# Transposing the normalised activations by DMA instead of by TensorE, in the QKV stage of an attention and mixture-of-experts layer

## What is computed

```
h = layernorm(x)
q, k, v = split(h @ w_qkv + b_qkv)            # 16 heads of 64
q = elu(q) + 1 ;  k = elu(k) + 1
kv  = sum over tokens of k^T v                # per head, 64 x 64
z   = 1 / (q . sum over tokens of k)
x = x + ((q @ kv) * z) @ w_proj + b_proj
h = layernorm(x)
gates = sinkhorn((h @ router_w^T + router_b) / temperature), 3 iterations, top 2 of 8
x = x + sum over experts of gate * (relu(h @ wg) * (h @ wp)) @ wo
```

## Time and profile before

| | |
|---|---|
| time, median of 2 runs | 7586.61 us (7111.52 and 8061.7) |
| the profiled execution | 7111.29 us |
| its span, first to last instruction, slowest core | 7109.5 us |
| the other cores' spans | 7101.5 to 7107.5 us |
| TensorE busy | 6254.6 us (88%) |
| VectorE busy | 2794.3 us (39%) |
| ScalarE busy | 839.1 us (12%) |

### The profile page before, as it was taken

How to read it: one execution, slowest core, us unless ns; L and a number is a source line. 1 busy time by engine, 2 the same in 40 slices (tenths; PEclk the granted TensorE clock), 3 DMA queues, 4 the chain that set the end, 5 groups by cost and what they waited for, 6 DMA issues and landing times.

```text
span 7109.5 us, 77888 instructions; the slowest of 8 cores (7101.5 to 7109.5 us)
## 1 busy us (share of the span) xinstructions
PE 6254.6 (88%) x29238; PEld 2744.0 (39%) x29238; DVE 2794.3 (39%) x5085; ACT 839.1 (12%) x1390; POOL 165.5 (2%) x202
## 2 busy tenths in 40 slices
PE   4777655589999999999999998999999999999999
PEld 1222222234444444444444443444444444444444
DVE  3444444433333333333333333333333333333334
ACT  1111111111111111111111110111111111111110
POOL 0000000000000000000000000000000000000000
PEclk9888766689999999999999999999999999999999
DMA  4000111142222222222222244222222222222222
GB/s 80 24 21 24 36 54 54 54 89 36 36 36 36 36 36 36 36 36 36 36 36 36 36 81 85 36 36 36 36 36 36 36 36 36 36 36 36 36 36 66
DMA packets 192672, 298.65 MB, mean 42 GB/s; under 512 B 5930, under 2 KB 137002, under 8 KB 192306
## 3 DMA queue, kind: packets, MB, share of 16 engines
q0 software_dynamic: 169120, 209.75, 20.8%
q1 hardware_dynamic: 23186, 83.93, 3.5%
HBM read 469.84 MB, written 33.55 MB: 71 GB/s over the span
## 4 chain that ended last, share of the span: by engine, by line
PE 72%; DVE 13%; issue 8%; ACT 4%; DMA 2%; DVEq 0%; ACTq 0%; SPq 0%; POOL 0%; POOLq 0%
PE p3p L748 25%; PE p3g L743 25%; PE p3o L788 13%; DVE out_acc L803 8%; PE p1kv L336 3%; PE p2pr L540 2%; ACT rt L760 2%; DMA out<-out_acc 1%; PE p1q L393 1%; DMA rws<-router_w 1%; DVE h2T L482 1%; DVE h1T L320 1%; ACT acH L579 1%; PE p2tr L478 1%; PE p1kv L340 1%
## 5 line engine op out<-in xcount | busy, mean ns | idle before, releaser
L788 PE MATMUL p3o<-wo_p,t 128*128 128x512 bf16 x8192 | 1853.5, 379 | 290.6 <-DVE out_acc L803 290.6
L743 PE MATMUL p3g<-h2T,wg_p 128*128 128x512 bf16 x8192 | 1936.9, 379 | 0.6 <-DVE sk L667 0.6
L748 PE MATMUL p3p<-h2T,wp_p 128*128 128x512 bf16 x8192 | 1935.8, 379 | 0.0
L770 DVE TENSOR_TENSOR t<-rt,p3p 128x512 bf16<-128x512 f32 x1024 | 703.8, 687 | 3023.1 <-ACT rt L760 3023.0
L803 DVE SCALAR_TENSOR_TENSOR out_acc<-p3o,wsel,out_acc 128x512 f32<-128x512 f32 x2048 | 1480.8, 747 | 447.7 <-PE p3o L788 335.0
L788 PEld LDWEIGHTS p3o<-wo_p,t 128*128 128x128 bf16 x8192 | 783.5, 98 | 1319.0 <-issue 413.6
L760 ACT ACTIVATE rt<-p3g 128x512 f32<-128x512 f32 x1024 | 611.5, 597 | 5012.5 <-PE p3p L748 5012.5
L743 PEld LDWEIGHTS p3g<-h2T,wg_p 128*128 128x128 bf16 x8192 | 801.9, 98 | 967.9 <-issue 2.4
L748 PEld LDWEIGHTS p3p<-h2T,wp_p 128*128 128x128 bf16 x8192 | 801.9, 98 | 967.2 <-issue 1.4
L336 PE MATMUL p1kv<-wqkv_sb,h1T 128*128 128x512 bf16 x1024 | 300.1, 445 | 34.9 <-DVE h1T L320 18.5
L196 POOL DMA_DIRECT2D wg_p<-wg x64 | 57.0, 890 | 5986.5 <-DVE out_acc L803 5343.8
(11 more groups left out here) (116 smaller groups left out, 1276.0 us busy)
## 6 DMA issues: line engine op xcount, KB each, us to landing
wg_p<-wg POOLq DMA_DIRECT2D x64, 1024.0 KB, 11.2
wp_p<-wp POOLq DMA_DIRECT2D x64, 1024.0 KB, 17.2
wo_p<-wo POOLq DMA_DIRECT2D x64, 1024.0 KB, 22.1
xt<-x SPq DMA_DIRECT2D x64, 512.0 KB, 3.8
base_scr<-xt SPq DMA_DIRECT2D x32, 512.0 KB, 2.7
out_acc<-base_scr SPq DMA_DIRECT2D x32, 512.0 KB, 8.6
out<-out_acc SPq DMA_DIRECT2D x32, 512.0 KB, 4.3
wqkv_sb<-w_qkv POOLq DMA_DIRECT2D x1, 6144.0 KB, 44.1
```

What stands on the lines that cost most here:

```text
L743: EM(T, lambda t, b=b, k=k, fsub=fsub, w=w, q=q, it3=it3: t.matmul(p3g[it3 % 2][:], wg_sb[b][:, 512 * k + 128 * fsub:512 * k + 128 * (fsub ...
L748: mmfn = lambda t, b=b, k=k, fsub=fsub, w=w, q=q, it3=it3: t.matmul(p3p[it3 % 2][:], wp_sb[b][:, 512 * k + 128 * fsub:512 * k + 128 * (fsu ...
L770: EM(V, lambda v, qt=qt, fsub=fsub, it3=it3: v.tensor_tensor(t_sb[qt][:, 512 * fsub:512 * (fsub + 1)], rt_sb[it3 % 2][:], p3p[it3 % 2][:], ...
L788: mmfn = lambda t, qt=qt, s4=s4, fsub=fsub, b=b, dmh=dmh: t.matmul(p3o[s4][:], t_sb[qt][:, 512 * fsub + 128 * s4:512 * fsub + 128 * (s4 + 1)],
```

## The change

The 8 TensorE transposes and 8 DVE copies of a subtile are replaced by 8 DMA transposes of 128 x 128 bf16, SBUF to SBUF, issued from SP's queue. SP waits until `h1b(i)` has been written and, from the second block on, until the last q matmul of the block before has been done, because `h1T` has one buffer. The semaphores that `p1_kvkvx` and `p1_ln_s` wait for are now two DMA semaphores, one for even and one for odd subtiles. The loop is reordered: the matmuls of subtile `i` (and the q groups) come first, then the layernorm and the transposes of subtile `i+2`; those of subtiles 0 and 1 stand ahead of the loop.

```diff
-    stpd = [SM["tpf"], SM["tpf"]]
+    stpd = [SM["tpd"], SM["tpd1"]]
...
     def p1_tr(i):
         sup, s4 = divmod(i, 4)
-        W(T, SM["h1"], i + 1)
+        W(SY, SM["h1"], i + 1)
+        if sup >= 1:
+            W(SY, SM["q"], 8 * sup)
         for j in range(8):
-            tp = i * 8 + j
-            if tp >= 2:
-                W(T, SM["tpf"], p1tpf_hist[tp - 2])
-            EM(T, lambda t, j=j, tp=tp, i=i: t.transpose(p1tr[tp % 2][:], h1b[i % 2][:, 128 * j:128 * (j + 1)],
-                                                         identb[:]).then_inc(SM["tp"].h, 1))
-            inc(SM["tp"])
-            W(V, SM["tp"])
-            EM(V, lambda v, j=j, tp=tp, s4=s4: v.tensor_copy(
-                h1T[:, 512 * j + 128 * s4:512 * j + 128 * (s4 + 1)],
-                p1tr[tp % 2][:]).then_inc(SM["tpf"].h, 1))
-            p1tpf_hist.append(inc(SM["tpf"]))
-        tpd_hist.append((i % 2, SM["tpf"].v))
+            dma(SY, h1T[:, 512 * j + 128 * s4:512 * j + 128 * (s4 + 1)],
+                h1b[i % 2][:, 128 * j:128 * (j + 1)], stpd[i % 2], tr=True)
+        tpd_hist.append((i % 2, stpd[i % 2].v))
...
     p1_ln_s(1)
+    p1_tr(0)
+    p1_tr(1)
     for i in range(NSUB):
-        if i + 2 < NSUB:
-            p1_ln_v(i + 2)
-        p1_tr(i)
-        if i + 2 < NSUB:
-            p1_ln_s(i + 2)
         p1_kvkvx(i)
         if i % 4 == 3:
             p1_q(i // 4)
+        if i + 2 < NSUB:
+            p1_ln_v(i + 2)
+            p1_ln_s(i + 2)
+            p1_tr(i + 2)
```

More of the change, by code:

```diff
@@ L257, in build_program @@
         inc(SM["sktf"])
-    stpd = [SM["tpf"], SM["tpf"]]
+    stpd = [SM["tpd"], SM["tpd1"]]
     tpd_hist = []
-    p1tpf_hist = []
     qf_hist = []
```

## The result

The changed kernel takes 7170.66 to 7171.9 us where the kernel before takes 7110.0 to 7111.5 us, and 7145.5 us once; the ratio of the comparable executions is 1.0073, 95% interval 1.0042 to 1.0103. By the 2% bound that is no change, but the interval lies above 1.

The account below looks back on a forecast made before the run. Phase 3, most of the time, was taken as TensorE at full clock and untouched; phase 1 would be limited by SP's queue: 256 x 1.68 - 280 = +150 us on 7111.3, so 7261 us, range 7000 to 7620.

Parts of the forecast that it names:

- a chain through SP's queue: Phase 1: transposes, next load, statistics, h1b, next transposes follow without slack; 8.0 us plus eight transposes' time per subtile.
- 4 I + 58.7 us: Phase 1, end of one block's q groups to the next: four subtiles' transposes plus 58.7 us, against 91.8 before.
- I: Time eight transposes of a subtile take of SP's queue or the DMA engines, whichever is longer; forecast 13.4 us.
- 32 I - 280 us: Change in whole time, seven later blocks plus the first, with 32 subtiles' transposes on SP; forecast +150 us.
- The price of a transpose: Time t of one DMA transpose on SP's queue or the DMA engines, estimated from neighbours at 1.68 us.
- I take the middle, 1.68 us: One DMA transpose put between 8 packets per engine, 1.12 us, and 16, 2.24 us, reading and writing paid separately.
- The rival with t near 1.12 us: Phase 1: transposes cost 8 packets per engine, overlapping issue; +7 us, 7118 us; chance 0.30 with the edge case.
- As cheap as a copy: SP needs 0.33 us per transpose issue and the engines keep up: 179 us saved, 6932 us; chance 0.08.
- Tile by tile: Hardware builds each transpose from small squares, t towards 3.9 us: 7599 us at 3.0, 7829 at 3.9; chance 0.23.
- The wait at the edge alone: Loads overtake transposes, only block edges pay: 129 us against savings up to 151; no change, within the 0.30.
- The 2.7: At a block's edge, landing of the last transpose after its issue: 2.7 us, the shortest issue to landing on this queue.
- Hand-over: Phase 1, from a subtile's load issue through landing, statistics and h1b to its transposes on SP: 8.0 us.

Follow-up runs that it names:

- e6_halves: Changed kernel with each 128 x 128 DMA transpose cut into two of 64 tokens x 128 channels, same bytes: 7483.3 us.
- e1_twice: Changed kernel with every DMA transpose issued twice, the second into a spare tile that nothing reads: 7488.6 us.
- e2_loads_pool: Changed kernel with the loads of xt issued from GpSimd's queue instead of SP's: spans of 7040 to 7047 us on cores 0 to 3.
- e7_before_grouped: Kernel before, with transposes and copies ahead of the later subtile's statistics, and four transposes into one PSUM tile with one copy out: 6977.9 to 6979.0 us.

## Why the prediction was right and wrong

- **The direction and the mechanism: right.** The time was to be decided by a chain through SP's queue, in blocks of 4 I + 58.7 us. With the I that was measured, 10.3 us, this gives 99.9 us a block; measured 100.6. The sum 32 I - 280 gives +50 us; measured +58.6 on the spans: 0.7 us more in each of seven blocks, and 150.0 instead of 147.2 us for the first. Doubling I moved the time by 318 us where the slope says 32 x 10.3 = 330.
- **The price of a transpose: wrong, and the size of the forecast with it.** The step that failed is "I take the middle, 1.68 us". It took the price to be that of the data's packets, 8 to 16 for each engine at 0.140 us. The queues' rows of the changed kernel show what was wrong with that:

```profile
q0 software_dynamic: 169120, 209.75, 19.3%
q1 hardware_dynamic: 64146, 92.35, 4.2%
```

Against the earlier trace rows the hardware queue has 40960 packets more, 160 for each transpose, 10 for each engine; the count was about right. It is nearer to the 8 of one pass over the rows than to the 16 of two; that reading and writing can't run as one stream was my assumption, and no run shows it. But its share rises only from 3.5% of 16 x 7109.5 us to 4.2% of 16 x 7168.1 us, 836 us for 40960 packets: 0.02 us each, not 0.14. By this the engines need 0.2 us for a transpose. What costs is the instruction, 1.23 us for either size (e6_halves), and no row of before shows one. The lower bound from a plain copy's issue, 0.33 to 0.38 us, was right as a bound; my middle was 0.39 us above the 1.29 measured, and at 256 transposes that is 100 us. The forecast was 91 us too high, 7261 instead of 7170, because the other terms of the sum were some 9 us short.
- **The rival with t near 1.12 us came nearer than the forecast.** Its band of 0.54 to 1.65 us, everything within 2%, holds the result. That its t of 1.12 us lies near the 1.29 is luck: it is eight packets at 0.140 us, and the packets take 0.02. That they pass while the next transpose is issued is so: eight transposes keep the queue 10.3 us, though each takes 2.3 us from issue to landing.
- **As cheap as a copy: ruled out.** A plain load took 0.33 us of SP's queue before and 0.52 us right behind transposes; a transpose of a sixteenth of its bytes takes 1.23 us. The data alone is cheap (0.2 us of the engines' time, by the queue's share), but 128 x 128 pieces issued one by one are not. No run here has a larger one.
- **Tile by tile: ruled out** by e6_halves, in which half the size costs the same.
- **The wait at the edge alone: ruled out** by e1_twice and e2_loads_pool.
- **The small terms.** From the end of the last transpose's issue to TensorE's start: 1.3 us instead of 2.7. The 2.7 was the whole time from issue to landing of a 512 KB store; a transpose's is 2.3, of which 1.2 is its issue, which I already counts. Hand-over 8.3 instead of 8.0. The last subtile's matmuls and the q groups together 33 (what is left of 100.6) instead of 32.0: the statistics between two evacuations, which I costed at nothing, do hold up the third group (1.66 and 2.42 us in the timeline) once the load is late; with the load in time they don't (e2_loads_pool). These three nearly cancel.
- **What I said one would see.** No `p1tr` for `h1b` on TensorE and 256 fewer copies: seen, VectorE has 4829 instructions against 5085. That the mean clock of phase 1 falls below 0.84: not seen, it is 0.84 again. TensorE waits for a DMA ahead of the k, v matmuls (169.6 us over the seven blocks) and takes the first group in 3.57 us; VectorE waits for `xt` (233.6 us). Within the wait at an edge the clock row shows both levels:

```profile
451.50:454.00 2.50, 0.00 (x0) 0.00 (x0) 1.53 (x3) 0.63 (x1) 0.00 (x0) 1.00 0.08 15
...
457.00:460.00 3.00, 0.00 (x0) 0.00 (x0) 0.00 (x0) 0.00 (x0) 0.00 (x0) 0.50 0.13 25
...
463.10:466.70 3.60, 3.60 (x9) 1.07 (x9) 0.90 (x2) 0.00 (x0) 0.00 (x0) 0.50 0.41 137
...
473.00:476.00 3.00, 2.71 (x11) 0.89 (x10) 1.23 (x3) 0.00 (x0) 0.00 (x0) 1.00 0.12 22
```

The granted clock is 1.00 when the wait begins, 0.50 later in it and through the first group, then 1.00. Before, it was 0.50 as well in the first group behind the transposes of subtile 17 (3.57 us), and 0.91 in the next 3 us:

```profile
456.30:460.00 3.70, 3.67 (x9) 1.11 (x9) 0.00 (x0) 1.11 (x1) 0.00 (x0) 0.50 0.28 71
460.00:463.00 3.00, 2.65 (x10) 0.81 (x9) 1.45 (x3) 0.63 (x1) 0.00 (x0) 0.91 0.22 87
```

So one slow group for each subtile replaces another.

## What to carry to other kernels

In this kernel a DMA transpose cost the issuing queue 1.3 us, at 128 x 128 and at half of that alike. So count instructions times that price, and see what else stands behind them on that queue: here the load that fed the next subtile did, and moving it to another queue gave 17.8 us a block. Taking work off an engine pays nothing when its replacement makes the path from one iteration to the next longer: write down that path and sum it before comparing busy times. Of the four ways in which TensorE's transposes were placed here, the fastest had them between two groups of long matmuls, with one copy for four of them and a second buffer for their target.

## What the runs showed that I had not expected

- A DMA transpose's time on SP's queue was the same for the two sizes tried: 1.228 us for 64 x 128, 1.232 us for 128 x 128.
- Right behind DMA transposes, SP took 0.52 us to issue a plain load, against 0.33 us before. In phase 2 of the same changed kernel, with no transposes on the queue, it is 0.33 us again.
- Regrouping the copies (e7_before_grouped) gave 77 us, more than twice what I had worked out from the waits: more than half of it is TensorE's own busy time, with the clock at 0.94 instead of 0.86.
